# Conv block on one core: late cells in another order, side steps moved, the input's halo copies issued by SP, evictions of the last body shared

## The chip, the cores and the metric

The kernel runs on one core of a Trainium2 chip. The metric is the device time of one execution in microseconds, shorter being better. The figures below come from three timed runs and from one more execution that the hardware profiler recorded.

## The reference

The input x is (8, 16, 112, 112) in float32. Four stages follow each other, each as x = x + stage(gn(x)), where gn is a group norm with 8 groups of 2 channels:

```
x = x + attention(gn(x))      # 4x4 windows, 16 heads of width 1, qkv and proj over 16 channels, relative bias
x = x + conv3x3(gn(x))        # 16 -> 16 channels ("conv1")
x = x + grid(gn(x))           # 4 x 4 grid of cells, 3x3 convolutions
x = x + quantised_conv3x3(gn(x))  # scale from the largest |x| of all images: needs every image first
```

The grid is the bulk of the work. Cell (col, row) convolves up to three inputs of 16 channels with its own weights, adds a bias, applies relu and splits 48 channels into three outputs:

```
for col in range(4):
    for row in range(4):
        if col == 0:   ins = [input] if row == 0 else [outs[row-1].down]
        elif row == 0: ins = [outs[0].right, outs[1].up]
        elif row == 3: ins = [outs[3].right, outs[2].down]
        else:          ins = [outs[row].right, outs[row+1].up, outs[row-1].down]
        outs[row] = relu(conv3x3(ins, W[col, row]) + b[col, row])   # right, up, down
result = outs[3].right
```

## The kernel before

**Tiles.** Everything stays in on-chip memory, one image at a time. A "pair" tile P[r] holds two inputs of row r (a RIGHT and an UP output, or DOWN in P[3]); a "half" tile S[k] holds one input, and S[2] holds the grid's or conv1's normalised input (INPUT). Image rows are folded into partitions, so a tile needs halo rows: after an output has been evicted, SP copies rows inside the tile by DMA, with two copies of 392 KB for one half of a pair tile (send_pair, L471 and L472) and six (four of 192 KB, two of 7 KB) for a half tile (send_half, L440 to L443).

**Units.** Each output that is used (O = D, U or R for DOWN, UP, RIGHT) of a cell is made in two units (0 and 1). A unit is a run of matmuls into two of four PSUM banks (L800 from the pair tile, L813 from the half tile, L790 for cell (3,3)), that ends with an increment of conv_done, and an eviction with bias and relu by ScalarE (L662), that increments relu_done. A unit with pair and half input takes PE 6.4 us, one with a pair alone 4.2 us, one of column 0 2.2 us. Unit k needs the banks of unit k - 2. For the cells in SHARED_MID VectorE evicts half of each unit (empty, L985, vec_relu_done). ScalarE evicts a unit in four pieces, or in eight shorter ones where a half tile is written and the cell also reads one.

**Bodies.** The program is a software pipeline over images: body m runs the late cells of image m and the early cells of image m + 1, while attention of image m + 2 runs between them. Body -1 has early cells only (50 units), bodies 0 to 4 are one hardware loop (sp.Fori, pe.Fori and so on, 68 units each), bodies 5 and 6 are written out behind it, and body 7 has late cells only (18 units). BODY is the order of the cells; a 1 marks a late cell. Of units 0 to 67, 0 to 13 are (2,2), (3,0), (2,3), (3,1) in some order, 14 to 17 are (0,0), 18 and 19 (3,2), 20 to 25 (0,1), 26 and 27 (3,3), 28 to 33 (0,2), 34 to 37 (1,0), 38 to 41 (0,3), 42 to 47 (1,1), 48 to 53 (1,2), 54 to 57 (2,0), 58 to 61 (1,3), 62 to 67 (2,1).

**Side steps.** Four tables per engine (FIRST for body -1, MID, BEFORE for body 5, LATE and LAST) say before which unit an engine does a step of attention, statistics or conv1. On PE these are qkv (three matmuls per chunk into side_banks), proj, mean and var (sums over partitions), and the two halves of conv1 (L728, side_banks). ScalarE has qkv (copy out of PSUM) and exp. SP has "xb" and "xa" (loads of the next image for the residual and for attention), "x3" (store of a finished image) and "last" (seven loads of 784 KB for the last stage, L495). Each engine works its list strictly in order: SP goes through the units, does the side steps of unit k, then waits for relu_done of the second unit of an output and issues its copies.

**VectorE.** Each body has 14 half chunks j of attention: scores(j + 1), then weigh(j) (softmax sums, product with v, division), with the shares of (0,0) to (0,3) behind weigh(4) to weigh(7), finish (statistics of image m) behind weigh(6), and at the end turn(): last residual, statistics, normalised conv1 input (normalise_stream, c_ready), then chunk 0 for the next body. The next body begins with scores(0) and add_conv1. GpSimd (POOL) computes the reciprocal roots (rstd_of) and before the change also issued the halo copies of INPUT (send_input), on its own queue.

The functions that the change touches, with their callers:

## Time and profile before

| | us |
|---|---|
| timed runs, median of 3 | 3408.66 (3399.5 to 3409.45) |
| profiled execution, its own time | 3410.37 |
| profiled execution, span | 3408.5 |
| mean granted clock of TensorE, share of full speed | 0.943 |

The span runs from the first to the last instruction. In the rows below PE is TensorE's matmuls, PEld its weight loads, DVE VectorE, ACT ScalarE, POOL GpSimd, and SPq a DMA being issued by SP. L12 is line 12 of the kernel. A timeline row gives the start, the time from there to the end of the group, the instruction, how many of them, and in brackets how long the engine sat idle before it and what ended that. A row of busy time by window gives the window, its length, the busy time of PE, PEld, DVE, ACT and POOL with their instructions, the mean granted clock (1.0 is full speed), the busy share of the DMA engines and what they moved in GB/s. To find a unit in the timeline, count the groups of matmuls that end with an increment of conv_done: 50 for body -1, 68 for each of bodies 0 to 6. Body 2, from which most rows are taken, runs from 1374.5 to 1747.9 us.

### The profile page before, as it was taken

The numbers are of one execution on the slowest core, as the hardware profiler recorded it, in microseconds if no ns is written. First come the engines' busy times: TensorE is split into PE (matmuls) and PEld (weight loads), VectorE is DVE, ScalarE is ACT, GpSimd is POOL, SyncE is SP. The second block draws the span as 40 slices with busy tenths as digits, with TensorE's granted clock in tenths as the row PEclk, the third lists the DMA queues.
The fourth block names the chain that finished last, engine by engine and source line by source line (L and its number), as shares of the span: only waits on it lengthen the run. The fifth ranks groups of instructions, "written<-read, shape, count | busy, mean of one in ns | idle before, by whom it ended". The sixth has DMA issues, their size and how long they took to land.

```text
span 3408.5 us, 87866 instructions
## 1 busy us (share of the span) xinstructions
PE 2939.4 (86%) x39580; PEld 1258.6 (37%) x39580; DVE 2238.6 (66%) x1962; ACT 2071.0 (61%) x2353; POOL 70.3 (2%) x163
## 2 busy tenths in 40 slices
PE   5775698988989899889988898989998999999943
PEld 5773233333333333333333333333333333333311
DVE  6565994779856994969676995789587961230013
ACT  1010976576757666666757675767667675767623
POOL 0001000000000000000000000000000000000000
PEclk9887898999989999999999999999999999999977
DMA  3011656576646756666737755575666664775566
GB/s 58 0 10 19 86 73 82 68 96 94 80 68 83 104 68 82 78 87 96 94 51 91 110 68 82 73 95 83 83 87 87 96 82 63 101 101 77 77 115 118
DMA packets 95703, 269.69 MB, mean 79 GB/s; under 512 B 79824, under 2 KB 80592, under 8 KB 83408
## 3 DMA queue, kind: packets, MB, share of 16 engines
q1 hardware_dynamic: 92240, 251.02, 54.4%
q0 software_dynamic: 3072, 12.85, 2.5%
q8 instruction: 320, 5.24, 0.8%
q14 instruction: 71, 0.58, 0.1%
HBM read 23.01 MB, written 12.85 MB: 11 GB/s over the span
## 4 chain that ended last, share of the span: by engine, by line
issue 62%; PE 26%; DVE 7%; DMA 1%; POOL 1%; ACT 1%; SPq 1%; POOLq 0%; DVEq 0%; ACTq 0%
PE conv_banks L800 12%; PE conv_banks L813 6%; PE conv_banks L833 5%; DVE half L975 2%; PE conv_banks L886 1%; DMA half<-half 1%; DVE score_max L1008 1%; ACT half L662 1%; DVE pair L985 1%; PE conv_banks L790 1%; PE side_banks L728 1%; DVE half L985 1%; POOL half L440 0%; DVE scores L1000 0%; DVE scores L998 0%
## 5 line engine op out<-in xcount | busy, mean ns | idle before, releaser
L662 ACT ACTIVATE pair<-conv_banks,b_cells 32x784 f32<-32x784 f32 x1340 | 1256.8, 938 | 618.8 <-PE conv_banks L813 533.5
L800 PE MATMUL conv_banks<-pair,w_cells 128*32 128x392 f32 x17664 | 1552.5, 501 | 13.3 <-ACT half L662 8.7
L813 PE MATMUL conv_banks<-half,w_cells 64*32 64x392 f32 x18432 | 903.2, 520 | 184.2 <-DVE half L985 42.3
L800 PEld LDWEIGHTS conv_banks<-pair,w_cells 128*32 128x32 f32 x17664 | 534.3, 109 | 972.8 <-issue 911.2
L662 ACT ACTIVATE half<-conv_banks,b_cells 32x392 f32<-32x392 f32 (+1 forms) x792 | 536.4, 677 | 184.5 <-PE conv_banks L813 149.3
L813 PEld LDWEIGHTS conv_banks<-half,w_cells 64*32 64x32 f32 x18432 | 343.9, 109 | 725.2 <-issue 698.0
L985 DVE TENSOR_SCALAR half<-conv_banks,b_cells 32x392 f32<-32x392 f32 x168 | 105.3, 626 | 259.2 <-PE conv_banks L813 256.6
L998 DVE TENSOR_TENSOR scores<-qkv 128x1792 f32<-128x1792 f32 x106 | 214.1, 2020 | 86.6 <-issue 48.7
L648 ACT ACTIVATE scores<-scores 128x1792 f32<-128x1792 f32 x106 | 180.1, 1699 | 112.6 <-DVE scores L1010 110.9
L985 DVE TENSOR_SCALAR pair<-conv_banks,b_cells 32x784 f32<-32x784 f32 x196 | 202.7, 1034 | 57.4 <-PE conv_banks L813 54.1
L1008 DVE TENSOR_REDUCE score_max<-scores 128x112 f32<-128x1792 f32 x106 | 214.1, 2020 | 9.8
L1010 DVE TENSOR_TENSOR scores<-scores,score_max 128x1792 f32<-128x1792 f32 x106 | 214.7, 2025 | 3.6
L1000 DVE TENSOR_TENSOR scores<-scores,rel_bias_sb 128x1792 f32<-128x1792 f32 x106 | 214.6, 2025 | 3.6
L1024 DVE TENSOR_TENSOR scores<-scores,qkv 128x1792 f32<-128x1792 f32 x98 | 198.4, 2025 | 3.4
L1027 DVE TENSOR_REDUCE score_max<-scores 128x112 f32<-128x1792 f32 x98 | 198.0, 2020 | 3.4
L1126 DVE TENSOR_TENSOR stream<-pair,stream 128x1568 f32<-128x1568 f32 x8 | 14.3, 1792 | 281.3 <-ACT pair L659 281.1
L1022 DVE TENSOR_REDUCE softmax_sum<-scores 128x112 f32<-128x1792 f32 x98 | 197.2, 2012 | 0.8
L643 ACT ACTIVATE qkv<-side_banks 128x672 f32<-128x672 f32 x56 | 40.9, 731 | 254.9 <-PE side_banks L761 132.7
L761 PE MATMUL side_banks<-att,w_qkv_sb 128*128 128x224 f32 x336 | 86.1, 398 | 62.2 <-issue 31.4
L833 PE MATMUL conv_banks<-scores,pair 128*128 128x112 f32 x512 | 102.6, 375 | 23.6 <-DVE att L1062 21.1
L833 PEld LDWEIGHTS conv_banks<-scores,pair 128*128 128x128 f32 x512 | 99.3, 229 | 25.9 <-issue 22.7
L728 PE MATMUL side_banks<-half,w_conv 64*32 64x392 f32 x768 | 80.8, 572 | 25.7 <-DMA half<-half 23.7
(90 smaller groups left out, 1193.6 us busy)
## 6 DMA issues: line engine op xcount, KB each, us to landing
pair<-pair SPq DMA_DIRECT2D x384, 391.9 KB, 8.6
half<-half SPq DMA_DIRECT2D x288, 192.4 KB, 5.2
half<-half POOLq DMA_DIRECT2D x64, 192.4 KB, 8.8
x_block<-in_x SPq DMA_DIRECT2D x64, 98.0 KB, 5.8
stream<-in_x SPq DMA_DIRECT2D x64, 98.0 KB, 5.1
x_scratch<-stream SPq DMA_DIRECT2D x8, 784.0 KB, 6.3
pair<-x_scratch SPq DMA_DIRECT2D x8, 784.0 KB, 15.3
out_dram<-pair SPq DMA_DIRECT2D x32, 196.0 KB, 4.3
```

The lines of the kernel that those rows point to most:

```text
L662: done = nc.scalar.activation(dst, src, ACT.Relu, bias=b_ap)
L800: done = nc.tensor.matmul(conv_ps[32 * q:32 * q + 32, n + b, 0:QN], w, P[row][:, QG * s:QG * (s + 1), QX * q + kx:QX * (q + 1) + kx], star ...
L813: done = nc.tensor.matmul(conv_ps[32 * q:32 * q + 32, n + h, 0:QN], w_all[rows, at:at + 32], T[rows, QG * u:QG * (u + 1), QX * q + kx:QX * ...
L833: done = nc.tensor.matmul(first_sum(kind, j), eye, e[:, :, b], start=b == 0, stop=b == WPX - 1)
L985: done = nc.vector.tensor_scalar(dst, src, b_ap, 0.0, ALU.add, ALU.max)
L998: ch.inc(nc.vector.tensor_tensor(e4, q, key, ALU.mult))
L1000: ch.inc(nc.vector.tensor_tensor(e, e, relb[:].unsqueeze(1).to_broadcast([BP, SW, WPX * WPX]), ALU.add))
L1008: ch.inc(nc.vector.tensor_reduce(m[:], ea, AX.X, ALU.max))
L1010: nc.vector.tensor_tensor(ea, ea, row_max(m), ALU.subtract).then_inc(scores_ready, 1)
L1022: side.inc(nc.vector.tensor_reduce(den[:], ea, AX.X, ALU.add))
L1024: side.inc(nc.vector.tensor_tensor(e4, e4, v, ALU.mult))
L1027: side.inc(nc.vector.tensor_reduce(mx[:], ea, AX.X, ALU.add))
```

## The change

- The late cells run as (3,0), (2,2), (3,1), (2,3) where they ran as (2,2), (3,0), (2,3), (3,1). The side steps of all engines get new places; near the body's end they stand two units later.
- SP issues the halo copies of INPUT, as side steps "conv1" and "input" (d is the image's offset), on the queue that all other copies use; POOL keeps only rstd. "xb" is loaded at the end of the body before, not at unit 4; "xa" of the first body moves from unit 40 to 30.
- In turn() the spread of image i + 1 stands ahead of normalise_stream. VectorE's share of (0,3) stands ahead of weigh(7).
- In the last body VectorE shares the evictions of all cells but (3,3). vec_value counts these too.

The diff, cut to its core (the tables left out change as their neighbours do):

```diff
-BODY = [((2, 2), 1), ((3, 0), 1), ((2, 3), 1), ((3, 1), 1), ((0, 0), 0), ((3, 2), 1), ((0, 1), 0), ((3, 3), 1),
+BODY = [((3, 0), 1), ((2, 2), 1), ((3, 1), 1), ((2, 3), 1), ((0, 0), 0), ((3, 2), 1), ((0, 1), 0), ((3, 3), 1),
...
-PE_MID = {0: [("qkv", 1, 0)], 4: [("proj", 0, 0), ("qkv", 2, 0)], 10: [("proj", 1, 0), ("qkv", 3, 0)],
-          27: [("proj", 2, 0), ("qkv", 4, 0)], 43: [("proj", 3, 0), ("qkv", 5, 0)],
-          48: [("proj", 4, 0), ("qkv", 6, 0)], 52: [("proj", 5, 0)], 57: [("proj", 6, 0)], 58: [("mean1", 0, 0)],
-          59: [("var1", 0, 0), ("mean0", 0, 1)], 60: [("var0", 0, 1)], 62: [("qkv", 0, 1)],
-          63: [("conv1", 0, 1)], 64: [("conv1", 1, 1)], 65: [("mean2", 0, 1)], 66: [("var2", 0, 1)]}
+PE_MID = {2: [("qkv", 1, 0)], 7: [("proj", 0, 0), ("qkv", 2, 0)], 12: [("proj", 1, 0), ("qkv", 3, 0)],
+          27: [("proj", 2, 0), ("qkv", 4, 0)], 44: [("proj", 3, 0), ("qkv", 5, 0)],
+          49: [("proj", 4, 0), ("qkv", 6, 0)], 54: [("proj", 5, 0)], 59: [("proj", 6, 0)], 60: [("mean1", 0, 0)],
+          61: [("var1", 0, 0), ("mean0", 0, 1)], 62: [("var0", 0, 1)], 64: [("qkv", 0, 1)],
+          65: [("conv1", 0, 1)], 66: [("conv1", 1, 1)], 67: [("mean2", 0, 1), ("var2", 0, 1)]}
...
+PE_BEFORE = {2: [("qkv", 1, 0)], 7: [("proj", 0, 0), ("qkv", 2, 0)], 12: [("proj", 1, 0), ("qkv", 3, 0)],
...
+             60: [("mean1", 0, 0)], 61: [("var1", 0, 0)], 64: [("conv1", 0, 1), ("conv1", 1, 1)],
+             65: [("mean2", 0, 1)], 66: [("var2", 0, 1)]}
...
+ACT_MID = {2: [("qkv", 1, 0), ("exp", 1, 0)], 5: [("exp", 2, 0)], 7: [("qkv", 2, 0), ("exp", 3, 0)],
+           9: [("exp", 4, 0)], 12: [("qkv", 3, 0), ("exp", 5, 0)], 19: [("exp", 6, 0)], 26: [("qkv", 4, 0)],
+           27: [("exp", 7, 0)], 38: [("exp", 8, 0)], 44: [("qkv", 5, 0), ("exp", 9, 0)], 47: [("exp", 10, 0)],
+           49: [("qkv", 6, 0), ("exp", 11, 0)], 51: [("exp", 12, 0)], 54: [("exp", 13, 0)], 64: [("qkv", 0, 1)],
+           65: [("exp", 0, 1)]}
...
-SP_FIRST = {6: ["xb"], 40: ["xa"]}
-SP_MID = {4: ["xb"], 34: ["x3"], 52: ["xa"]}
-SP_BEFORE = {4: ["xb"], 34: ["x3"]}
-SP_LATE = {34: ["x3"]}
-SP_LAST = {NL - 4: ["last"]}
...
-SHARED_MID, SHARED_LATE, SHARED_LAST = [(0, 0), (0, 1), (0, 2), (0, 3)], [(0, 0), (0, 1), (0, 2), (0, 3)], []
...
+SP_FIRST = {1: [("xb", 1), ("input", 0)], 30: [("xa", 2)], 44: [("conv1", 1)], 47: [("xb", 2)],
+            49: [("input", 1)]}
+SP_MID = {35: [("x3", -1)], 48: [("xa", 2)], 63: [("conv1", 1)], 66: [("xb", 2)], 67: [("input", 1)]}
+SP_BEFORE = {35: [("x3", -1)], 62: [("conv1", 1)], 67: [("input", 1)]}
+SP_LATE = {35: [("x3", -1)]}
+SP_LAST = {NL - 4: [("last", 0)]}
...
+SHARED_FIRST, SHARED_MID, SHARED_LATE, SHARED_LAST = [], [(0, 0), (0, 1), (0, 2), (0, 3)], [(0, 0), (0, 1), (0, 2), (0, 3)], [(3, 0), (2, 2), (3, 1), (2, 3), (3, 2)]
...
+            def send_input(i, which):
+                sp.wait_ge(c_ready, i * 2 * NQ + (which + 1) * NQ)
+                send_half(sp, INPUT)
...
             sp.wait_ge(zeroed, N_ZERO)
+            send_input(0, 0)
             body(-1)
...
-            def send_input(i, which):
-                pool.wait_ge(c_ready, i * 2 * NQ + (which + 1) * NQ)
-                pool.sem_inc(pool_held, 1)
-                send_half(pool, INPUT)
...
             with pool.Fori(0, B - 2) as b:
                 rstd_of(b, 2)
-                send_input(b, 1)
                 rstd_of(b + 1, 1)
-                send_input(b + 1, 0)
                 rstd_of(b + 2, 0)
...
                 spread(i, 1, ch, nm1)
+                if more:
+                    spread(i + 1, 0, ch, nm0)
                 normalise_stream(1, nm1, i, last_read)
                 if more:
-                    spread(i + 1, 0, ch, nm0)
                     normalise_chunk(i + 1, 0)
...
+                    if not early and j == 7:
+                        empty(m, [(0, 3)])
                     weigh(i, j)
-                    if not early:
-                        if 4 <= j < 8:
-                            empty(m, SHARED_MID[j - 4:j - 3])
-                        if j == 6:
-                            finish(m, m)
+                    if not early and j == 4:
+                        empty(m, [(0, 0)])
+                    if not early and j == 5:
+                        empty(m, [(0, 1)])
+                    if not early and j == 6:
+                        empty(m, [(0, 2)])
+                    if not early and j == 6:
+                        finish(m, m)
```

## Rows read from the trace of the kernel before

**Rows 1.** The page, parts 1, 5 and 6.
```profile
PE 2939.4 (86%) x39580; PEld 1258.6 (37%) x39580; DVE 2238.6 (66%) x1962; ACT 2071.0 (61%) x2353; POOL 70.3 (2%) x163
...
L662 ACT ACTIVATE pair<-conv_banks,b_cells 32x784 f32<-32x784 f32 x1340 | 1256.8, 938 | 618.8 <-PE conv_banks L813 533.5
...
pair<-pair SPq DMA_DIRECT2D x384, 391.9 KB, 8.6
```

**Rows 2.** Busy time by window: body 2, half-clock stretch, load ahead of conv1.
```profile
1374.50:1747.90 373.40, 339.89 (x4820) 132.19 (x4814) 287.86 (x248) 249.66 (x283) 7.52 (x15) 0.96 0.63 84
...
1472.70:1476.30 3.60, 3.57 (x56) 1.94 (x64) 0.00 (x0) 2.29 (x4) 0.00 (x0) 0.60 0.85 137
...
1690.00:1706.00 16.00, 12.43 (x166) 4.79 (x155) 0.86 (x3) 11.75 (x16) 2.60 (x6) 0.99 0.96 149
```

**Rows 3.** Timeline at starts of bodies 3 and 5 (start, duration, idle before).
```profile
1755.73 2.60 PE L761 MATMUL side_banks<-att,w_qkv_sb 128*128 128x224 f32 x6 [7.83 <-issue]
...
2495.32 1.40 PE L761 MATMUL side_banks<-att,w_qkv_sb 128*128 128x224 f32 x6
...
1705.70 2.03 DVE L998 TENSOR_TENSOR scores<-qkv 128x1792 f32<-128x1792 f32 x1 [11.89 <-issue]
```

**Rows 4.** Timeline, body 2: TensorE and ScalarE up to (0,0).
```profile
1440.37 4.23 PE L800 MATMUL conv_banks<-pair,w_cells 128*32 128x392 f32 x48 [1.29 <-ACT half L662]
...
1465.39 4.26 PE L813 MATMUL conv_banks<-half,w_cells 64*32 64x392 f32 x96
1472.73 5.92 PE L813 MATMUL conv_banks<-half,w_cells 64*32 64x392 f32 x96 [3.08 <-ACT half L662]
...
1461.40 4.84 ACT L662 ACTIVATE half<-conv_banks,b_cells 32x392 f32<-32x392 f32 x8 [1.02 <-PE conv_banks L813]
```

**Rows 5.** Timeline, body 2: TensorE, ScalarE and VectorE at (0,3).
```profile
1564.82 2.25 PE L813 MATMUL conv_banks<-half,w_cells 64*32 64x392 f32 x48 [1.69 <-ACT pair L662]
1571.92 5.92 PE L813 MATMUL conv_banks<-half,w_cells 64*32 64x392 f32 x96 [4.86 <-DVE pair L985]
1577.89 2.56 PE L800 MATMUL conv_banks<-pair,w_cells 128*32 128x392 f32 x28
...
1566.42 3.78 ACT L662 ACTIVATE pair<-conv_banks,b_cells 32x784 f32<-32x784 f32 x4
...
1562.46 2.01 DVE L1022 TENSOR_REDUCE softmax_sum<-scores 128x112 f32<-128x1792 f32 x1
...
1569.69 4.20 DVE L985 TENSOR_SCALAR pair<-conv_banks,b_cells 32x784 f32<-32x784 f32 x4
```

**Rows 6.** Timeline: input's copies on GpSimd, conv1 in bodies 2 and 5.
```profile
1689.11 0.54 POOL L440 DMA_DIRECT2D half<-half  x1 [5.67 <-DVE half L975]
...
1705.97 5.64 PE L728 MATMUL side_banks<-half,w_conv 64*32 64x392 f32 x48 [3.57 <-DMA half<-half]
...
2812.96 4.22 PE L728 MATMUL side_banks<-half,w_conv 64*32 64x392 f32 x48 [3.11 <-DMA half<-half]
```

**Rows 7.** Timeline, TensorE: first body at (1,3) R, body 0 at ("proj", 0).
```profile
570.26 0.59 PE L710 MATMUL stat_bank<-meanvar,g_all_sb 128*128 128x2 f32 x2 [14.02 <-DVE meanvar L931]
...
571.21 6.39 PE L800 MATMUL conv_banks<-pair,w_cells 128*32 128x392 f32 x48
...
660.54 1.61 PE L771 MATMUL stat_bank<-att,w_proj_sb 128*128 128x112 f32 x8 [3.70 <-DVE att L1029]
```

**Rows 8.** Timeline, VectorE before its share of (0,0), body 2.
```profile
1469.76 2.55 DVE L985 TENSOR_SCALAR half<-conv_banks,b_cells 32x392 f32<-32x392 f32 x4 [21.50 <-PE conv_banks L813]
```

**Rows 9.** Timeline, last body: SP's queue and TensorE.
```profile
3254.13 0.51 SPq L440 DMA_DIRECT2D half<-half  x1
...
3259.71 3.43 SPq L495 DMA_DIRECT2D pair<-x_scratch  x7
...
3263.24 4.17 PE L813 MATMUL conv_banks<-half,w_cells 64*32 64x392 f32 x48 [9.92 <-DMA half<-half]
...
3297.03 11.11 PE L790 MATMUL conv_banks<-pair,w_cells 128*32 128x392 f32 x96 [22.57 <-issue]
```

More of the change, by code:

```diff
@@ L183 @@
-PE_BEFORE = {0: [("qkv", 1, 0)], 4: [("proj", 0, 0), ("qkv", 2, 0)], 10: [("proj", 1, 0), ("qkv", 3, 0)],
-             27: [("proj", 2, 0), ("qkv", 4, 0)], 43: [("proj", 3, 0), ("qkv", 5, 0)],
-             48: [("proj", 4, 0), ("qkv", 6, 0)], 52: [("proj", 5, 0)], 57: [("proj", 6, 0)],
-             58: [("mean1", 0, 0)], 59: [("var1", 0, 0)], 63: [("conv1", 0, 1), ("conv1", 1, 1)],
-             64: [("mean2", 0, 1)], 65: [("var2", 0, 1)]}
+PE_MID = {2: [("qkv", 1, 0)], 7: [("proj", 0, 0), ("qkv", 2, 0)], 12: [("proj", 1, 0), ("qkv", 3, 0)],
[3 more added lines that the diff above has]
+          65: [("conv1", 0, 1)], 66: [("conv1", 1, 1)], 67: [("mean2", 0, 1), ("var2", 0, 1)]}
@@ L222, in vec_value @@
 def vec_value(m, k):
-    per = sum(cell in SHARED_MID for cell, _, _ in UNITS)
+    ahead, per = n_shared(-1, NF), sum(cell in SHARED_MID for cell, _, _ in UNITS)
     if not isinstance(m, int):
-        return m * per + n_shared(m, k + 1)
-    return max(min(m, B - 2), 0) * per + (n_shared(B - 2, NB) if m == B - 1 else 0) + n_shared(m, k + 1)
+        return m * per + ahead + n_shared(m, k + 1)
+    if m < 0:
+        return n_shared(m, k + 1)
+    return ahead + min(m, B - 2) * per + (n_shared(B - 2, NB) if m == B - 1 else 0) + n_shared(m, k + 1)
 def sides(m, first, mid, before, late={}, last={}):
```

42 lines of the change are left out of this document (19 added, 23 removed).

## The prediction

> **What bounds the kernel now.** I read the page first: the matmul engine, PE, is busy 86% of the span and nothing else comes near it [rows 1]. So the time is PE's work plus PE's holes, and I looked for the holes: busy time by body, then PE's timeline, counting units by the matmuls that end a unit. A middle body takes 373 us with 340 busy [rows 2]. The reader should see three kinds of hole: jumps of the loop, single waits of 1 to 5 us that repeat at the same unit of each body, and two long waits at the two ends of the program. Around some holes the granted clock halves: at 1472.7 its mean is 0.60, which is a mix of 2.4 and 1.2 GHz [rows 2]; there 96 matmuls of (0,0) take 5.92 us, where 96 of the same shape took 4.26 just before [rows 4]. I price such a half-clock stretch at 1.4 to 1.7 us.
>
> **Part 1: what the change cannot reach.** PE idles 7.8 us at the start of bodies 1 to 4, before the matmuls of ("qkv", 1). All that these wait for was ready earlier. At the start of body 5, which is written out behind the loop, the same matmuls follow with no gap; VectorE too has an idle "issue" of 11.9 us at its own jump [rows 3]. I therefore take the 7.8 us for the jump backwards and not for a wait of the step that moves from unit 0 to unit 2: no gain from that move. The Trainium skill (Advanced Engine Details and Errata, Control Flow Timing) gives 51 ns for a branch and 108 ns for a compare and branch; by that alone the hole would be a wait, and the move would cover it. The trace disagrees, and the measurement stands; the case is a rival below.
>
> **Part 2: the late cells and (0,0), per body.** Before, ("exp", 4) sits in front of an eviction between units that give PE 4.2 us, and PE waits 1.3 us at 1440.4. Then (3,1) D, whose eviction takes 8 pieces, 4.84 us, stands right ahead of (0,0), whose units give PE only 2.2 us: 3.1 us at 1472.7 [rows 4]. After, (2,3) R stands there. Its eviction is 4 x 938 ns = 3.8 us [rows 1], and the second (0,0) unit needs it two units back: 3.9 - 2.2 = 1.7 us idle. Counting ScalarE through (3,1) and (2,3) with ("exp", 4) before the second of (3,1) (6.6 us of eviction and exp against 6.4 of PE), one wait of 1.0 stays. So 4.4 becomes 2.7, and after so short a hole I expect no half clock (holes of 1.7 us at 1564.8 cost none, [rows 5]): 1.7 + 1.7 = **3.4 us a body**. Bounds: 0.9, if the clock still falls and half the idle stays, and 6.1, if all of it goes.
>
> **Part 3: VectorE's share of (0,3).** PE waits 4.9 us at 1571.9 for VectorE, which runs weigh(7), 7.2 us, before it evicts (0,3) from 1569.7 on [rows 5]. Moved ahead of weigh(7) the eviction starts when the first (0,3) unit ends, 1563.1. ScalarE becomes the limit: its eviction of that unit ends at 1568.3 in this trace, so R starts 3.5 us sooner and at full clock, and (1,1) starts at 1573.2 where it was 1577.9: **4.7 us a body**, bounds 3.5 and 5.5. The stall does not come back: VectorE leaves (0,3) about 3 us later than now and ("proj", 3) needs weigh(7) at unit 44, by my count still 3 us after it is done; at the end of attention VectorE waits for ("proj", 6) now, and that step moves two units back.
>
> **Part 4: conv1 and the input's halo copies.** Now POOL issues six copies from 1689.1 and PE starts conv1 at 1706.0 after 3.6 us idle, at a reduced clock (5.64 us; 4.22 in body 5) [rows 6]. VectorE waits for POOL's pow, queued behind these issues; that ends, but is hidden before and after by its own jump. In the new order SP issues the copies behind the two of (1,3) R. With E the end of unit 61: eviction to E+3.9, two issues to E+5.1, VectorE's normalised stream at E+6.3 (the second spread now stands ahead of it and waits for var0 at unit 62), six issues. Landing alone takes 9.1 us (3254.1 to 3263.2, [rows 9]), so E+15 if the copies overlap wholly. If they share the engines as the two queues do now, 16.9 us: E+23. By bytes, 784 KB of pair copies and 784 KB of half copies at the 149 GB/s of 1690 to 1706 [rows 2] need 10.5 us from E+7: E+17.5; I take **E+19.5**, nearer the upper row. PE reaches conv1 at E + 3 x 6.4 + qkv 1.3 + 0.5 = E+21: no wait. New is var2 directly behind mean2 at unit 67: PE idles about 1.1 us while VectorE does three short instructions. Gain 3.6 (4.0 in other bodies) + 1.4 - 1.1 = **4.0 us a body**; bounds -1 (landing at E+23 and half clock) and 5.
>
> The Trainium skill (DMA: Bandwidth & Descriptors, Queues, rings and completion order) says that each DMA engine takes turns between queues and works one queue in order. It speaks against this edit: in the common queue the input's copies lose their turn to the pair copies. Its order alone, by the 149 GB/s, gives the E+17.5 above. No row of before shows a half copy issued right behind a pair copy.
>
> **Part 5: the bodies where conv1 is not covered.** In the first body conv1 stands three steps behind unit 43 (E+14.1), in body 5 two units behind unit 61 (E+13.1). With halos at E+19.5 PE waits 5.4 and 6.4 us, plus 1.4 of half clock each. First body: the wait of 14.0 us for the x block at 570.3 goes, because SP now issues that load at unit 30, some 50 us sooner; unit 42 too returns from 6.4 to 4.2: 14.0 + 2.2 - 6.8 = **9.4 us**. Body 0: the 3.7 us before ("proj", 0) [rows 7] go, since it stands about 8 us of conv further back: **3.7 us**. Body 5: 3.4 + 4.7 + 3.1 - 6.4 - 1.4 = **3.4 us**.
>
> **Part 6: VectorE later at the start of a body.** ("qkv", 1) behind (3,0) makes scores(2) some 13 us later relative to PE. It waits 21.5 us at (0,0) now [rows 8]; with 2.5 more for ("qkv", 2), 6 to 8 us of cover stay. Cost nothing; without the cover each us is lost in every body. (3,1) now stands two units behind (2,2) U: its copies land at 3.9 + 0.55 (an issue) + 8.6 [rows 1] = 13.1 us, PE arrives after 12.8 + 2.2. Nothing in the middle bodies. (3,0) at once behind (2,1) needs a copy with the same 13.1: bodies 6 and 7 lose about 1.5 each, body 5 less. Body 6: 0.9 idle + 1.4 - 1.5 = **0.8 us**.
>
> **Part 7: the last body.** PE waits 9.9 us for the halo of (3,1), then 22.6 for that of (3,2) [rows 9]. The second is not the halo's own time: seven loads of 784 KB are issued at 3259.7 and the halo goes behind them; together they need to 3297.0, 37.3 us. VectorE's share halves the evictions (3.8 to 2.2), and (2,3) now hides the halo of (3,1). With S the start: (2,3) ends S+75.4, the loads go out at S+79.1 behind the R copies (S+87), and the last halo lands at about S+118.5. Now it is S+123.2. The gain is 4.6 - 1.5 = **3.1 us**, though PE saves far more; bounds -1 and 9.
>
> **Sum.** 9.4 + 3.7 + 5 x (3.4 + 4.7 + 4.0) + 3.4 + 0.8 + 3.1 = 80.9 us. The profiled execution took 3410.4 (span 3408.5 and 1.9 around it), 1.7 above the median of the runs; 3410.4 - 80.9 - 1.7 = **3328 us**.
>
> **Rivals.** (A) The hole at the jump is a wait of the moved step: 4 x (7.8 + 1.5) more, 3291. For it: the matmuls behind the hole are just these. Against it: bodies 0 and 5. (B) The input's copies land late in every body, at E+23 or more, or half clocks stay: 20 to 30 us less, 3348 to 3358. For it: 16.9 us now; against it: the lighter load at that place. (C) Slower than before: VectorE, started 13 us later, is late at (0,0) in each body. It decides from about 7 us beyond what I counted, and cancels the whole gain at 81 / 6 = 13.5 more: 3420 at 22 us beyond. Against it: from scores(2) to (0,0) VectorE waits for little but ("qkv", 2), so it can slip no further than it starts late. (D) No change: the holes move and their sum stays, 3405; it needs B and half of C together.
>
> **Chances.** Forecast (3310 to 3344) 0.58, A 0.08, B 0.20, between B and D 0.05, D 0.04, C 0.05. A measurement of this kernel tells about 0.3%, 10 us. The range 3300 to 3362 takes in the bounds of parts 2 to 4 times five where they do not all fall together, and B; it leaves out A, C and D. Faster 0.91, same 0.04, slower 0.05.
>
> **What would show it.** In the profile of the changed kernel: the 7.8 us "issue" still at four body starts, now before (3,0); about 1.7 us idle at the second (0,0) unit; no VectorE wait above 2 us at (0,3); conv1 with no wait in bodies 0 to 4 and with 5 to 6 us in the first and in body 5; no 14 us wait in the first body; some 25 us before (3,3). A wait at (3,1) or at (0,0) for VectorE would make the forecast wrong.

## The result, and the profile after

The changed kernel takes **3323.86 us**, median of 4 runs (3321.67 to 3326.64), against 3409.05 for the kernel before in the same session (4 runs, 3399.5 to 3410.18): a ratio of 0.9757, 95% interval 0.9738 to 0.9776 (times are medians here and below, ratios are of means). The forecast was 3328 us with a range of 3300 to 3362. That the total is so close is partly luck, which the lengths of the bodies show. A body ends with the last matmul of its last unit; the lengths are those of the windows between these ends.

| body | before, us | after, us | measured | forecast |
|---|---|---|---|---|
| -1 | 629.9 | 623.0 | -6.9 | -9.4 |
| 0 | 369.4 | 353.5 | -15.9 | -15.8 |
| 1 to 4, each | 373.4 to 375.3 | 358.3 to 358.5 | -14.9 to -16.9 | -12.1 |
| 5 | 359.1 | 361.5 | +2.4 | -3.4 |
| 6 | 319.4 | 320.3 | +0.9 | -0.8 |
| 7 | 134.3 | 134.3 | 0 | -3.1 |
| behind the last body | 100.4 | 98.6 | -1.8 | 0 |

Bodies 1 to 4 gave 62.4 us where 48.4 were forecast; all the rest gave 21.2 where 32.5 were. The two errors nearly cancel.

The changed kernel's page, parts 1, 3, 5 and 6, to be read beside [rows 1]:

```profile
PE 2919.7 (88%) x39580; PEld 1250.6 (38%) x39580; DVE 2272.9 (68%) x1998; ACT 2042.5 (61%) x2317; POOL 23.2 (1%) x67
...
q1 hardware_dynamic: 95312, 263.86, 59.2%
q8 instruction: 320, 5.24, 0.9%
...
L662 ACT ACTIVATE pair<-conv_banks,b_cells 32x784 f32<-32x784 f32 x1316 | 1235.7, 939 | 604.8 <-PE conv_banks L813 539.7
...
half<-half SPq DMA_DIRECT2D x352, 192.4 KB, 5.4
```

PE does the same 39,580 matmuls in 19.7 us less, because fewer of them run at the lower clock: by the trace's clock records it is busy at that level for 149 us where it was 202. ScalarE's evictions have gone to VectorE in the last body only (the row of [rows 1] has 24 instructions more). Part 3 has a line that the forecast should have used: queue q8 carries instructions, and part 3 counts its packets on the same DMA engines as the copies'.

Busy time by window: body 2 to set against [rows 2], the stretch behind the second (0,1) unit, the one behind the jump, and conv1 in body 5 (columns: window, its length, PE's busy time with its matmuls, granted clock, DMA share, GB/s).

```profile
1334.90:1693.40 358.50, 336.15 (x4819) 0.99 0.66 87
...
1450.90:1454.40 3.50, 3.46 (x48) 0.62 1.05 115
1338.70:1342.30 3.60, 3.57 (x24) 0.55 1.47 180
2734.50:2740.70 6.20, 6.11 (x48) 0.67 0.60 100
```

Of body 2's 14.9 us, 3.7 is PE's busy time (339.89 to 336.15) and 11.2 is holes (33.5 to 22.3). Timeline of PE in body 2 of the changed kernel: the jump, (0,0), (0,1), (0,3), (1,1) and conv1.

```profile
1338.73 2.54 PE L800 MATMUL conv_banks<-pair,w_cells 128*32 128x392 f32 x16 [3.80 <-issue]
...
1426.91 2.25 PE L813 MATMUL conv_banks<-half,w_cells 64*32 64x392 f32 x48 [1.78 <-ACT pair L662]
...
1450.91 3.46 PE L813 MATMUL conv_banks<-half,w_cells 64*32 64x392 f32 x48 [2.02 <-ACT pair L662]
...
1517.05 2.25 PE L813 MATMUL conv_banks<-half,w_cells 64*32 64x392 f32 x48 [1.67 <-ACT pair L662]
1520.78 4.26 PE L813 MATMUL conv_banks<-half,w_cells 64*32 64x392 f32 x96 [1.48 <-ACT pair L662]
...
1536.04 0.89 PE L813 MATMUL conv_banks<-half,w_cells 64*32 64x392 f32 x15
1538.47 1.84 PE L813 MATMUL conv_banks<-half,w_cells 64*32 64x392 f32 x33 [1.54 <-issue]
...
1664.84 4.21 PE L728 MATMUL side_banks<-half,w_conv 64*32 64x392 f32 x48
```

What the reader is to see: the hole at the jump is 3.8 us, where [rows 3] had 7.8; (0,0) waits 1.8 us at full clock, where [rows 4] had 3.1 and a half clock; (0,3) waits 1.5 for ScalarE, where [rows 5] had 4.9 for VectorE; conv1 has no wait, where [rows 6] had 3.6. Two things are new: a half clock at (0,1) and 1.5 us in the middle of one unit of (1,1), where PE waits for nothing that the profile names.

The ends of the program, timeline: conv1 in the first body and in body 5, then SP's queue and PE in the last body ([rows 9] before), where PE waits 29.6 us for the copies of (3,2), issued behind the seven loads.

```profile
586.28 6.79 PE L728 MATMUL side_banks<-half,w_conv 64*32 64x392 f32 x48 [6.09 <-DMA half<-half]
...
2734.59 6.13 PE L728 MATMUL side_banks<-half,w_conv 64*32 64x392 f32 x48 [7.31 <-DMA half<-half]
...
3171.71 0.51 SPq L472 DMA_DIRECT2D pair<-pair  x1
...
3172.97 9.53 SPq L505 DMA_DIRECT2D pair<-x_scratch  x7
...
3216.45 3.85 PE L790 MATMUL conv_banks<-pair,w_cells 128*32 128x392 f32 x24 [29.59 <-issue]
```

### The profile page after: what moved, and what is told of

It reads as the page before. It is cut to its first block, busy times and chain, and to the rows that moved or that the text cites. A ratio compares the mean times of both kernels' runs of the same rounds, so it can differ in the third digit from the quotient of the medians.

```text
span 3324.9 us, 87852 instructions
## 1 busy us (share of the span) xinstructions
PE 2919.7 (88%) x39580; PEld 1250.6 (38%) x39580; DVE 2272.9 (68%) x1998; ACT 2042.5 (61%) x2317; POOL 23.2 (1%) x67
## 3 DMA queue, kind: packets, MB, share of 16 engines
q8 instruction: 320, 5.24, 0.9%
## 4 chain that ended last, share of the span: by engine, by line
PE 71%; DVE 10%; ACT 8%; issue 7%; SPq 1%; DMA 1%; POOL 0%; DVEq 0%; ACTq 0%; POOLq 0%
PE conv_banks L800 41%; PE conv_banks L813 19%; PE conv_banks L833 5%; ACT pair L662 4%; ACT half L662 3%; PE side_banks L728 2%; DVE half L985 2%; PE side_banks L761 1%; DVE pair L985 1%; PE stat_bank L771 1%; DVE score_max L1008 1%; ACT scores L648 1%; PE conv_banks L886 1%; DVE scores L1000 1%; DVE scores L998 1%
## 5 line engine op out<-in xcount | busy, mean ns | idle before, releaser
L662 ACT ACTIVATE pair<-conv_banks,b_cells 32x784 f32<-32x784 f32 x1316 | 1235.7, 939 | 604.8 <-PE conv_banks L813 539.7
L800 PE MATMUL conv_banks<-pair,w_cells 128*32 128x392 f32 x17664 | 1554.7, 501 | 40.2 <-issue 26.1
L662 ACT ACTIVATE half<-conv_banks,b_cells 32x392 f32<-32x392 f32 (+1 forms) x780 | 528.8, 678 | 200.9 <-PE conv_banks L813 139.0
L813 PEld LDWEIGHTS conv_banks<-half,w_cells 64*32 64x32 f32 x18432 | 335.0, 107 | 685.2 <-issue 651.9
L985 DVE TENSOR_SCALAR half<-conv_banks,b_cells 32x392 f32<-32x392 f32 (+1 forms) x180 | 114.4, 636 | 334.7 <-PE conv_banks L813 178.7
L985 DVE TENSOR_SCALAR pair<-conv_banks,b_cells 32x784 f32<-32x784 f32 x220 | 227.5, 1034 | 113.6 <-PE conv_banks L813 103.2
L833 PE MATMUL conv_banks<-pair 128*128 128x112 f32 x384 | 77.0, 376 | 24.9 <-DVE att L1062 24.9
L790 PE MATMUL conv_banks<-pair,w_cells 128*32 128x392 f32 x768 | 68.8, 508 | 30.6 <-issue 29.6
```

What stands on the lines that cost most here:

```text
L662: done = nc.scalar.activation(dst, src, ACT.Relu, bias=b_ap)
L800: done = nc.tensor.matmul(conv_ps[32 * q:32 * q + 32, n + b, 0:QN], w, P[row][:, QG * s:QG * (s + 1), QX * q + kx:QX * (q + 1) + kx], star ...
L813: done = nc.tensor.matmul(conv_ps[32 * q:32 * q + 32, n + h, 0:QN], w_all[rows, at:at + 32], T[rows, QG * u:QG * (u + 1), QX * q + kx:QX * ...
L833: done = nc.tensor.matmul(first_sum(kind, j), eye, e[:, :, b], start=b == 0, stop=b == WPX - 1)
L985: done = nc.vector.tensor_scalar(dst, src, b_ap, 0.0, ALU.add, ALU.max)
```

## The experiments

Twelve further kernels ran, in four sessions; in each the kernel before ran beside them (medians 3404.5 to 3410 us). A ratio is always to the kernel before. The changed kernel itself ran in the first session only, so a difference to it of a few us between medians is weak, and the bodies of the two profiles are the better measure.

### What sets the hole at the jump

**Moving the step alone, in the kernel before.**

```diff
-PE_MID = {0: [("qkv", 1, 0)], 4: ...
+PE_MID = {2: [("qkv", 1, 0)], 4: ...       # PE_BEFORE and ACT_BEFORE alike
-ACT_MID = {0: [("qkv", 1, 0), ("exp", 1, 0)], 2: [("exp", 2, 0)], ...
+ACT_MID = {2: [("qkv", 1, 0), ("exp", 1, 0), ("exp", 2, 0)], ...
```

> The kernel before with one edit, the counterpart: ("qkv", 1) with its exp goes from unit 0 to unit 2 of the bodies and nothing else changes. Theory (the place of the step): the hole at the start of bodies 1 to 4 falls from 7.8 to 3.7 us, and the time is 3409 - 16 = 3393 us. Rival (the surroundings): the hole stays at 7.8 us, now before the convolution matmuls of the first cell, and the time stays at 3409 us. Third way: the hole shrinks, but VectorE, which gets its second scores later, is late at (0,0), and 3409 comes back.

Measured: 3451.44 us (5 runs), ratio 1.0132 (1.0110 to 1.0155). Timeline of PE at the start of body 2, and at unit 4:

```profile
1392.92 0.88 PE L800 MATMUL conv_banks<-pair,w_cells 128*32 128x392 f32 x4 [7.85 <-issue]
...
1428.19 2.05 PE L771 MATMUL stat_bank<-att,w_proj_sb 128*128 128x112 f32 x8 [6.14 <-DVE att L1029]
```

The hole stays (7.85 to 8.24 us in bodies 1 to 4), now before the cell's matmuls, so it is no wait of ("qkv", 1): rival A of the forecast is out. And the move by itself costs 42 us. VectorE gets its scores later and is late for ("proj", 0) at unit 4, 6.1 us in each of bodies 0 to 5, with a half clock behind it (granted 0.55 over the 4.4 us from 1428.1). That is the mechanism of rival C, at another place than I had put it. In the change it does not bite because ("proj", 0) moves from unit 4 to 7 as well: in body 2 of the changed kernel VectorE has its input ready at 1368.7, which is 6.1 us behind the start of unit 4 and 12.9 us ahead of the step at its new place.

**The step back at unit 0, in the changed kernel.**

```diff
-PE_MID = {2: [("qkv", 1, 0)], ...
+PE_MID = {0: [("qkv", 1, 0)], ...          # PE_BEFORE, ACT_MID, ACT_BEFORE alike
```

> The changed kernel with one edit: the step ("qkv", 1) and its exp stand at unit 0 of the bodies again, first behind the loop's jump. In the kernel before PE had a hole of 7.8 us there, in the changed one 3.7 us. Theory (the place of the step): the jump alone costs the 3.7 us, the rest of the 7.8 comes with this step as the first thing behind the jump. Then the hole at the start of bodies 1 to 4 is 7 to 8 us again and the time is 3324 + 4 x 4.1 = 3340 us. Rival (the surroundings): the hole shrank because the input's copies are no longer issued from POOL just then, or because other cells stand there; then it stays at 3.7 us and the time is 3324 us, give or take 4.

Measured: 3335.18 us (5 runs), ratio 0.9783 (0.9761 to 0.9804). The time lies between the two, but the hole is the rival's, so the theory falls: at the jumps nothing changed.

```profile
1343.20 1.06 PE L761 MATMUL side_banks<-att,w_qkv_sb 128*128 128x224 f32 x3 [3.80 <-issue]
...
2428.09 1.25 PE L800 MATMUL conv_banks<-pair,w_cells 128*32 128x392 f32 x12 [3.81 <-ACT half L662]
```

The medians differ by 11 us, the two profiled spans by 8.5, and that comes in bodies 0 and 5 (359.4 and 364.9 us for 353.5 and 361.5), which no jump precedes: ScalarE now takes exp(1) ahead of an eviction and PE waits 3.8 us for that one at unit 2. Bodies 1 to 4 take 358.3 to 358.6 us and have no such wait; that the jump's hole gives ScalarE the time there fits, but was not tried.

**Fewer copies under way at the jump, in the kernel before.** POOL holds back the copies of the input's second halo until PE has done four units of the next body.

```diff
 def send_input(i, which):
     pool.wait_ge(c_ready, i * 2 * NQ + (which + 1) * NQ)
+    if which and not (isinstance(i, int) and i == 0):
+        pool.wait_ge(conv_done, unit_base(i - 1) + 4)
...
-with pool.Fori(0, B - 2) as b:
+with pool.Fori(1, B - 2) as b:      # the steps of b = 0 are written out ahead of it
```

> The kernel before with one edit: POOL holds back the copies of the input's second halo until PE has done four units of the next body (they are needed at unit 8), so that six copies fewer are under way when PE jumps back. The trace of before has these copies landing from 1375.7 to 1381.2, and PE's hole from 1374.5 to 1382.3. Moving the step ("qkv", 1) out of the way had left the hole as it was (7.85 us, before the matmuls of the cell). Theory (traffic): behind the jump the engine's next instructions come in behind the copies under way, so the hole shrinks to 4 us or less in bodies 1 to 4, and the time is 3409 - 4 x 4 = 3393 us or a little under. Rival (place of the code, or another order of cells): the hole stays at 7.8 us, the time at 3409 us.

Measured: 3394.88 us (12 runs), ratio 0.9964 (0.9949 to 0.9978). Timeline at the start of body 2, and the window of that body:

```profile
1376.14 1.11 PE L768 MATMUL side_banks<-att,w_qkv_sb 128*128 128x224 f32 x2 [3.99 <-issue]
```
```profile
1372.10:1744.20 372.10, 342.11 (x4821) 0.96 0.63 84
```

The hole falls from 7.86 to 3.99 us though PE's code and the place of every other step are the same: the copies under way set it. Less than that reaches the time, since bodies 1 to 4 take 1.3 to 3.5 us less each and not 3.9; in body 2 conv1 waits 0.5 us longer and PE is busy 342.1 us for 339.9.

**Still fewer, in the changed kernel.**

```diff
-SP_MID = {35: ..., 48: ..., 63: ..., 66: [("xb", 2)], 67: [("input", 1)]}
+SP_MID = {3: [("input", 0)], 5: [("xb", 1)], 35: ..., 48: ..., 63: ...}
```

> The changed kernel with one edit: the load of the x block (xb) goes from unit 66 to unit 5 of the next body and the copies of the input's second halo from unit 67 to unit 3, so that nothing but the copies of (2,1) is under way at the jump. Theory (traffic): PE's hole of 3.7 us at the start of bodies 1 to 4 shrinks further, to 1 to 3 us, and with it the half-clock stretch behind it may go (1.7 us): 3324 - 4 x 1 to 4 x 4 = 3308 to 3320 us. Rival: 3.7 us is what a jump costs with nothing under way, no change at the jump, 3324 us; it is slower than that only if the later x block or halo brings a wait of its own.

Measured: 3314.40 us (4 runs, 3304.42 to 3327.75), ratio 0.9725 (0.9698 to 0.9752), which overlaps that of the changed kernel. The hole is 2.7 to 3.1 us, and bodies 1 to 4 take 358.1 to 358.6 us in the profiled execution, as in the changed kernel. That execution was the slowest of the four, and it shows no gain; whether the faster ones have one is open. About 3 us is the least that any of these kernels had at the jump.

**What PE waits for at the jump.** The packed traces have each packet of q8 with its start and its end. The table gives body 2; "jump" is the end of the last matmul of body 1.

| kernel | copies of the input's second halo issued | packet of 16 KB starts, us behind the jump | lands | hole |
|---|---|---|---|---|
| before | all six 6.2 to 3.7 us ahead | 4.3 | 6.2 | 7.9 |
| order and all places of before (below) | four ahead, two behind | 3.1 | 4.9 | 6.7 |
| fewer copies, in the kernel before | none near | -0.1 | 2.2 | 4.0 |
| changed | one 0.4 us ahead, five behind | 0.1 | 1.9 | 3.8 |
| input's copies on POOL's queue (below) | all behind | 0.1 | 1.9 | 3.6 |
| still fewer, in the changed kernel | none near | -0.1 | 1.2 | 3.0 |

In all of them, and in bodies 1, 3 and 4, PE goes on 1.6 to 2.0 us after such a packet has landed. So the hole is the time of this packet plus a part that does not change, and what the half copies issued ahead of the jump cost is the time by which the packet starts later (1.4 us in body 3 of the second kernel of the table, 3.0 to 4.4 us else). What is issued at the jump or behind it adds little: 586 KB move during the hole of the changed kernel and almost nothing during that of the third kernel, and the holes differ by 0.2 us. Nor do the eight loads of the x block (98 KB each), which the changed kernel issues 12.8 to 2.5 us ahead of the jump, hold the packet back; why the half copies do and these do not is open.

### The late cells and the places of the steps

**Order and all places of before, the rest as changed.** BODY, PE_MID, PE_BEFORE, ACT_MID and ACT_BEFORE are those of before; SP sends the input's copies at units 63 and 67.

> The changed kernel with the late cells in the order of before, (2,2), (3,0), (2,3), (3,1), and all side steps of the middle bodies at the places of before; the input's copies stay in the common queue, the share of (0,3) ahead of weigh(7), the first body and the last body as changed, so this undoes parts 2 and 6 of the forecast and the 3.7 us of part 5 for body 0. Forecast's terms: 3.4 us a body in six bodies and 3.7 once come back, and var2 is no longer directly behind mean2 (-1.1 x 6): 3324 + 20 + 4 - 7 = 3341 us. Theory (traffic): the x block is loaded at unit 4 again, so fewer copies lie at the jump and its hole stays under 4 us. Rival (the order of the cells made the hole of 7.8 us): it returns, 3341 + 16 = 3357 us.

Measured: 3452.01 us (4 runs), ratio 1.0140 (1.0116 to 1.0163). Both expectations missed, by 111 and 95 us.

```profile
1720.84 1.53 PE L728 MATMUL side_banks<-half,w_conv 64*32 64x392 f32 x8 [12.24 <-DMA half<-half]
```

PE reaches conv1 two units earlier while SP still issues its copies behind those of (1,3) R, and waits 12.2 us in each of bodies 0 to 4 (13.5 in body 5), and 3.0 to 3.5 us for ("proj", 3) at unit 43, since weigh(7) now stands behind the share of (0,3). The edit mixed two things and says little of the order of cells. It does say what the later places are worth: with the common queue and the share as changed, but the steps where they were, the kernel is slower than before. At the jump the hole is 6.7 us in body 2: mean2 and var2 stand early again, and SP issues the input's second copies from 1375.2 on, across PE's jump at 1382.0 (timeline of SP's queue and of PE):

```profile
1375.22 1.91 SPq L441 DMA_DIRECT2D half<-half  x1
...
1388.70 0.74 PE L761 MATMUL side_banks<-att,w_qkv_sb 128*128 128x224 f32 x1 [6.73 <-issue]
```

**Only the late cells and the steps of units 0 to 12 put back.**

```diff
-BODY = [((3, 0), 1), ((2, 2), 1), ((3, 1), 1), ((2, 3), 1), ...
+BODY = [((2, 2), 1), ((3, 0), 1), ((2, 3), 1), ((3, 1), 1), ...
-PE_MID = {2: [("qkv", 1, 0)], 7: [("proj", 0, 0), ("qkv", 2, 0)], 12: [("proj", 1, 0), ("qkv", 3, 0)],
+PE_MID = {0: [("qkv", 1, 0)], 4: [("proj", 0, 0), ("qkv", 2, 0)], 10: [("proj", 1, 0), ("qkv", 3, 0)],
...                                          # PE_BEFORE, ACT_MID, ACT_BEFORE alike
```

> The changed kernel with only the late cells in the order of before, (2,2), (3,0), (2,3), (3,1), and the side steps of units 0 to 12 where they stood with that order; everything from unit 40 on stays as changed (the kernel with all steps put back had mixed this with conv1 two units too early). It undoes parts 2 and 6 and the gain of body 0. Forecast's terms: (0,0) idles 4.4 us with a half-clock stretch again in place of 2.7, 3.4 us a body in six bodies, and 3.7 us before ("proj", 0) in body 0: 3324 + 20 + 4 = 3348 us, less 3 for the halo waits that go in bodies 6 and 7: 3345 us. Rival (part 3 and part 2 were one gain): VectorE, started earlier, shortens its own waits further on and less than 10 us come back: 3332 us. On the hole at the jump: if it is set by the copies under way and not by the order of cells, it stays at 3 to 4 us; by the order rule it would be 7.8.

Measured: 3351.19 us (4 runs), ratio 0.9838 (0.9821 to 0.9856).

```profile
1346.49 0.83 PE L761 MATMUL side_banks<-att,w_qkv_sb 128*128 128x224 f32 x3 [3.81 <-issue]
...
1435.79 2.79 PE L813 MATMUL conv_banks<-half,w_cells 64*32 64x392 f32 x40 [3.09 <-ACT half L662]
```

It is 27 us slower than the changed kernel (22.6 by the two spans, in which its first body is 4.3 us shorter, from a place where no edit stands); the forecast's terms said 21. Bodies 1 to 3 take 361.6 us for 358.4, 3.2 us for a forecast of 3.4, and body 4 4.2. The hole at the jump stays 3.8 us, so the order of the cells has no part in it. The last body takes 130.9 us with the old order for 134.3 with the new: that term was missing from part 7.

### VectorE's share of (0,3)

```diff
-    if not early and j == 7:
-        empty(m, [(0, 3)])
     weigh(i, j)
+    if not early and j == 7:
+        empty(m, [(0, 3)])
```

> The changed kernel with one edit: VectorE takes its share of (0,3) behind weigh(7) again. Forecast's term: 4.7 us a body in six bodies, so 3324 + 28 = 3352 us, with PE waiting about 5 us at the third (0,3) unit and a half-clock stretch behind it. Rival, from the profile of the changed kernel: with the edit PE still idles 1.7 + 1.5 us at (0,3) and has a new hole of 1.8 us in (1,1), so that the share's place was worth only 4.9 + 1.5 - 3.2 - 1.8 = 1.4 us a body: 3332 us.

Measured: 3339.33 us (4 runs), ratio 0.9799 (0.9775 to 0.9823): 15.5 us more than the changed kernel, 2.6 a body (12.8 by the two spans), between the two expectations.

```profile
1526.24 5.91 PE L813 MATMUL conv_banks<-half,w_cells 64*32 64x392 f32 x96 [4.86 <-DVE pair L985]
```

The wait of 4.9 us and its half clock are back (5.91 us for 4.26), but the hole of 1.5 us in (1,1) is gone. That hole is PE's instructions coming in late: in body 2 of the changed kernel a packet of q8 lands at 1536.79 and PE goes on at 1538.47, 1.68 us behind it, as at the jump, and so in each body. A longer wait just ahead hides it: it is missing here, in the kernel before and in the kernel with three edits below, which all wait 4.5 to 6.5 us at (0,3).

### The queue of the input's copies

POOL issues the input's copies again, with its pow for the next image ahead of them; SP's two steps go.

```diff
 with pool.Fori(0, B - 2) as b:
     rstd_of(b, 2)
+    send_input(b, 1)
     rstd_of(b + 1, 1)
     rstd_of(b + 2, 0)
+    send_input(b + 1, 0)
```

> The changed kernel with the input's halo copies on POOL's own queue again (POOL does its pow for the next image ahead of them, since the second spread stands ahead of the stream). Theory (two queues share the DMA engines): the copies take 16.9 us from their issue as they did before, land at E+23 instead of E+19.3, and PE, at conv1 at E+21, waits 2 us and runs conv1 at half clock for 1.4 more in bodies 0 to 4: 17 us; the waits of the first body and of body 5 grow by 3.7 each: 3324 + 24 = 3348 us. Rival (the queue makes no difference): PE's order alone covers the copies, the same bytes land at the same time, 3324 us, give or take 4. Third way: a queue of their own lets them overtake the pair copies, the waits of 6.1 and 7.3 us in the first body and in body 5 get shorter and the others stay at nothing: 3316 us.

Measured: 3317.33 us (4 runs, 3314.5 to 3324.47), ratio 0.9731 (0.9707 to 0.9756), which overlaps the changed kernel's. Conv1 in the first body and in body 5:

```profile
585.05 2.79 PE L738 MATMUL side_banks<-half,w_conv 64*32 64x392 f32 x13 [4.31 <-DMA half<-half]
...
2729.20 2.19 PE L738 MATMUL side_banks<-half,w_conv 64*32 64x392 f32 x12 [4.22 <-DMA half<-half]
```

The third way: conv1 has no wait in bodies 0 to 4 with either queue, and where it is not covered its waits are 1.8 and 3.1 us shorter with a queue of its own. So the common queue did not end the wait before conv1. Nor did it shrink the hole at the jump, which is 3.6 us here too. POOL issues the input's second copies just as PE jumps (1334.24 and 1334.1), where in the kernel before they went out 6 us ahead of it (1368.37 and 1374.5), since mean2 now stands two units later and var2 one:

```profile
1334.24 0.54 POOL L441 DMA_DIRECT2D half<-half  x1 [5.60 <-DVE half L985]
```

### The two ends

**The x block late again in the first body, no sharing in the last.**

```diff
-SP_FIRST = {..., 30: [("xa", 2)], ...
+SP_FIRST = {..., 40: [("xa", 2)], ...
-SHARED_LAST = [(3, 0), (2, 2), (3, 1), (2, 3), (3, 2)]
+SHARED_LAST = []
```

> The changed kernel with two edits that lie 2,500 us apart and are read off the profile separately: the load of the next x block (xa) in the first body back from unit 30 to unit 40, and no sharing of evictions in the last body. Forecast's terms: the first body gets the wait of 14 us back and loses part of the 6.1 + 1.4 before conv1, 9.4 us in all less what the copies cost either way; the last body loses 3.1 us: 3324 + 12 = 3336 us. Theory from the profile of the changed kernel for the last body: the loads ahead of the halo copies of (3,2) set the end, which did not move (134.3 us before and after), so the sharing is worth 0 and the wait of 29.6 us only shrinks by what PE arrives later. Rival: sharing was worth the forecast's 3.1 us and something else took it; then the last body takes 137 us.

Measured: 3346.58 us (4 runs), ratio 0.9816 (0.9796 to 0.9836).

```profile
570.35 0.59 PE L710 MATMUL stat_bank<-meanvar,g_all_sb 128*128 128x2 f32 x2 [14.30 <-DVE meanvar L931]
```

The time lies 10.6 us above the expected 3336. The first body takes 638.6 us for 623.0: the earlier load was worth 15.6 us, and none of it came out of the wait before conv1 (6.09 us either way). The last body takes 137.5 us for 134.3. My theory of 0 falls and the rival holds: the sharing is worth 3.2 us, and the new order of cells takes that back (3.4 us, by the kernel with the late cells put back).

**The loads of the last body two units later.**

```diff
-SP_LAST = {NL - 4: [("last", 0)]}
+SP_LAST = {NL - 2: [("last", 0)]}
```

> The changed kernel with one edit: the seven loads of the last body are issued two units later, behind the halo copies of (3,2), in place of ahead of them. In the profile of the changed kernel these copies are issued at 3189.1 and land at 3216.4, behind the loads, and PE waits 29.6 us. Theory (the load queue bounds the last body): the copies land 10 us after their issue, PE's wait falls from 29.6 to 12 or 13 us, and the loads, 38 us from 3190, still land before their reader at 3260: 3324 - 17 = 3307 us. Rival: the loads then end late for the last stage, or the copies wait for other traffic, and less than 5 us is left.

Measured: 3317.09 us (4 runs), ratio 0.9741 (0.9718 to 0.9764). Timeline: PE at (3,3), and at the last stage.

```profile
3197.18 1.53 PE L790 MATMUL conv_banks<-pair,w_cells 128*32 128x392 f32 x8 [11.54 <-issue]
...
3261.16 1.28 PE L886 MATMUL conv_banks<-pair,w_cells 128*128 128x448 bf16 x3 [41.89 <-DMA half<-pair]
```

The wait falls from 29.6 to 11.5 us, so the loads were what it waited behind. The last stage then waits 41.9 us where the changed kernel waits 34.4: its small transfers now stand behind the loads. SP issues the next transfer 11.0 us after the store of the last rows (L500), where the changed kernel needs 3.3. So 17 us are gained and 8 lost, and the total lies 10 us above the expected 3307.

### What these point to

**Three edits together**: the loads in two lots, as soon as the tiles that they overwrite are read for the last time; the input's copies ahead of those of (1,3) R; the share of (0,2) ahead of weigh(6).

```diff
-SP_FIRST = {..., 44: [("conv1", 1)], ...
+SP_FIRST = {..., 43: [("conv1", 1)], ...
-SP_MID = {..., 63: [("conv1", 1)], ...
+SP_MID = {..., 61: [("conv1", 1)], ...       # SP_BEFORE: 61 for 62
-SP_LAST = {NL - 4: [("last", 0)]}
+SP_LAST = {2: [("last", 0)], 12: [("last", 1)]}      # four loads, then three
...
+    if not early and j == 6:
+        empty(m, [(0, 2)])
     weigh(i, j)
...
-    if not early and j == 6:
-        empty(m, [(0, 2)])
```

> The changed kernel with three edits. (1) The loads of the last body go in two lots as soon as their tiles are free, four behind (3,0) and three behind (3,1), so that neither the halo copies of (3,2) nor the last stage stand behind them: with the loads merely two units later PE's wait had fallen from 29.6 to 11.5 us, and 7.5 of these 18 came back in the last stage; now all 18 should stay. (2) SP sends the input's first halo copies ahead of the copies of (1,3) R: the wait for conv1 falls from 6.1 to 2 us in the first body and from 7.3 to 3 in body 5, nothing changes in the others: 8 us. (3) VectorE takes its share of (0,2) ahead of weigh(6), as it does (0,3): PE's wait of 4.5 us at the third (0,2) unit and the half clock behind it go, about 3 us of waits for ScalarE stay as at (0,3): 3 us a body in six bodies, 18 us. Together 3324 - 18 - 8 - 18 = 3280 us. Rivals: VectorE, idle before (0,2), ends later and PE waits at (0,3), no gain from (3), 3298 us; the loads now delay the copies of (2,2) and (3,1), and PE waits at (3,1) or (3,2) in the last body for 5 to 10 us of the 18.

Measured: **3291.16 us** (5 runs, 3290.65 to 3293.92), ratio 0.9662 (0.9647 to 0.9676). Timeline: the third (0,3) unit in body 2, conv1 in body 5, and (2,2) in the last body.

```profile
1507.47 2.87 PE L812 MATMUL conv_banks<-half,w_cells 64*32 64x392 f32 x32 [6.50 <-ACT pair L661]
...
2711.12 4.22 PE L727 MATMUL side_banks<-half,w_conv 64*32 64x392 f32 x48 [0.16 <-DMA half<-half]
...
3106.22 1.55 PE L812 MATMUL conv_banks<-half,w_cells 64*32 64x392 f32 x24
3110.86 1.74 PE L812 MATMUL conv_banks<-half,w_cells 64*32 64x392 f32 x24 [3.09 <-issue]
```

The copies ahead: both waits before conv1 go wholly, and with them the half clocks, which gives 9.0 us in the first body and 9.1 in body 5 at that place, 18 us for an expected 8. The bodies themselves shrink by more (609.9 us for 623.0, 349.8 for 361.5), but 4.2 us of the first come in its first 17 units, where no edit stands and where these kernels differ by up to 4.6 us among themselves, and 1.9 of body 5 in (1,1), whose hole is missing, as in the kernel before. The share of (0,2): nothing, the wait of 4.5 us turns up at (0,3) as 6.5 us, and bodies 1 to 4 take 358.3 to 358.7 us as before. The loads: 122.7 us for 134.3, and the last stage keeps its wait (34.9 us for 34.4). But with four loads under way PE stops for 3.1 us in the middle of one unit's matmuls. The total misses the expected 3280 us by 11: of the three terms of 18, 8 and 18 us, the loads gave 12, the copies 18 and the share none.

**The loads one at a time, the share of (0,2) left where it was.**

```diff
-SP_LAST = {NL - 4: [("last", 0)]}
+SP_LAST = {2: [("last", 0)], 4: [("last", 1)], 6: [("last", 2)], 8: [("last", 3)],
+           10: [("last", 4)], 12: [("last", 5)], 14: [("last", 6)]}
...                                          # "conv1" at 43 and 61 as with three edits
```

> The version that the runs point to: the changed kernel with SP sending the input's first halo copies ahead of the copies of (1,3) R (which took away both waits for conv1, 24.8 us in the profile of the kernel with three edits), the share of (0,2) back behind weigh(6) (moving it gave nothing in bodies 0 to 4), and the seven loads of the last body one every second unit instead of in lots of four and three (the four in a row left a hole of 3.1 us in the middle of PE's matmuls of (2,2), and (3,2) copies may have met the last of the three). Forecast by the place of each: first body and body 5 as in the kernel with three edits, bodies 0 to 4 as in the changed kernel, the last body 117 to 119 us: 3324 - 25 - 16 = 3283 us. Theory (PE's instructions are fetched by the same DMA engines as the copies): no hole over 1 us in the middle of (2,2) in the last body. Rival: the hole belongs to the order of the code there and stays; 3286 us. For the share of (0,2): if its place was worth nothing, bodies 0 to 4 take 358 us each, within 0.5 of both kernels.

Measured: 3291.98 us (5 runs), ratio 0.9675 (0.9657 to 0.9693), the same as with three edits and 9 us above the expected 3283.

```profile
3151.05 1.53 PE L800 MATMUL conv_banks<-pair,w_cells 128*32 128x392 f32 x8 [5.37 <-issue]
```

The stop in (2,2) is gone, so it belonged to the four loads and not to the code. It too ended behind a packet of q8, which landed at 3109.19 for matmuls at 3110.86. In its place PE waits 5.4 us at (3,2), for 3.3 in the changed kernel, since the copies of (2,3) U need 10.6 us beside the loads for 8.6, and the last body takes 121.4 us. Bodies 1 to 4 take 356.4 to 358.6 us, so the share's place is worth nothing there.

## Why the prediction was right, and where it was not

**The total.** Of its parts the late cells and the x block came out as forecast, the share of (0,3) was put too high, conv1 too low, and the jump at nothing. In bodies 1 to 4 the parts now measured add up to what is seen: 4.1 us at the jump, 3.4 for the late cells, 2.6 for the share and 5.2 for conv1 are 15.3 a body, for a mean of 15.6. The forecast had 0, 3.4, 4.7 and 4.0. Without the 16 us of the jump the changed kernel would have taken 3340 us, inside the range still, but not within 5 us of the forecast.

**The jump (part 1): right that it is no wait of the step, wrong that 7.8 us are out of reach.** Two kernels show that the step has no part in it, one that the order of cells has none, and two that the copies under way have. The page gives q8 320 packets and 5.24 MB, 16.4 KB each, and 66 bytes for each of PE's 79,160 matmuls and weight loads; that q8 is PE's own queue is read from this. The Trainium skill (Runtime: NRT & Kernel Launch, Instruction fetch mechanics) says that an engine gets its instructions over a DMA queue of its own in blocks of 16 KiB, and that a taken branch outside its window forces a fetch; the packets and the holes of the table above agree. With the pair copies and all six half copies issued ahead of the jump it cost 7.8 to 8.2 us, with some of the six behind it 5.2 to 6.7, with at most one ahead 3.3 to 4.0, with next to nothing under way 2.7 to 3.1. Because the change sends the input's second copies later, it gained 4 us in each of four bodies that I had ruled out, 16 us in all, more than the 14 by which bodies 1 to 4 beat the forecast. The argument by body 5, which has no jump and no hole, showed where the hole belongs and not that it is fixed.

**The late cells (part 2): right.** The terms 4.4 to 2.7 us of idle came out as 4.4 to 2.9, the half clock at (0,0) went, and putting the cells back costs 3.2 us a body in bodies 1 to 3. Not foreseen: (0,1) has a half clock now (48 matmuls in 3.46 us), behind the same 2.0 us of idle as before, which takes back what the next unit's wait lost.

**The share of (0,3) (part 3): right mechanism, 4.7 us mis-sized; 2.6 by the experiment.** Up to the start of (1,1) body 2 gains 4.9 us, as forecast. The step that failed is "the stall does not come back": 1.5 to 1.8 us return in (1,1) in bodies 0 to 4, not as a wait for VectorE, which I had looked for, but as instructions that come in late.

**Conv1 and the queue (part 4): 4.0 forecast; the rows of body 2 give 3.6 + 1.4 - 0.6 = 4.4,** and the mean of bodies 1 to 4 is 5.2, since bodies 1 and 3 of the kernel before had a half clock of 2.7 us there where body 2 had 1.4. In body 1 the copies landed 19.3 us behind E, the end of unit 61, for E+19.5. But the margin was thin (PE reaches conv1 1 us behind that), and the gain is that of the places: it is there with either queue. Where conv1 is not covered, the input's copies cost 1.8 and 3.1 us more behind the pair copies in one queue than in their own, and ahead of them nothing is left to wait for. By the rule of the Trainium skill that the forecast weighed (DMA: Bandwidth & Descriptors, Queues, rings and completion order) they lose their turn there; these runs agree.

**First body and body 0 (part 5): 9.4 and 3.7.** The x block was worth 15.6 us for a forecast of 16.2; the wait for conv1 is 6.1 and its half clock 2.6 (6.79 for 4.21 us), for 5.4 and 1.4. Body 0 came out to 0.1 us by errors that in part cancel: 2.3 us for the share in place of 4.7, 5.9 for conv1 in place of 4.0, 8.9 for the late cells and ("proj", 0) in place of 7.1. **Body 5: 3.4 us forecast, 2.4 us lost.** Conv1 waits 7.3 us for a forecast of 6.4 with half clock (6.13 us), the share of (0,3) gave less as above, and idle times at (3,2) and at (1,1), 1.1 and 1.0 us, are new. What of the 5.8 us belongs to which of these was not separated.

**Bodies 6 and 7 (parts 6 and 7).** The halo waits at (3,0) and (3,1) were 1.8 and 1.9 us in body 6, where I had one of 1.5. In the last body I had the copies of (3,2) at 118.5 us behind its start S; they let PE go on at 3216.45, S+124.4. The loads go out at S+81.0 for S+79.1, and 43.5 us pass from there for the 39.4 I had taken: the copies of (2,3) R, 1.3 us ahead of the loads, were not priced with them.

## What to carry to other kernels

At a loop's jump look at which transfers are issued just ahead of it before calling the hole fixed: here putting one lot of six copies off by four units halved it. In a common queue look at what a small transfer stands behind: the halves that PE waits for first belong ahead of the pairs that it needs later, which was worth 18 us here where changing the queue was worth 7 at most. And try a step's move with its followers: moved alone, one step cost 42 us in a set of moves that together gained.
